# A graph pass's destination scores in fp32 with eight columns per step, instead of three bf16 parts

## The reference, cut to what matters

```
hh = (x @ W).reshape(n, H, D)
s_src = jnp.einsum('nhd,hd->nh', hh, a_src)
s_dst = jnp.einsum('nhd,hd->nh', hh, a_dst)
scores = jax.nn.leaky_relu(s_src[src] + s_dst[dst], negative_slope=0.2)
m = jax.ops.segment_max(scores, dst, num_segments=n)
e = jnp.exp(scores - m[dst])
denom = jax.ops.segment_sum(e, dst, num_segments=n)
out = jax.ops.segment_sum(hh[src] * (e / denom[dst])[:, :, None], dst, num_segments=n)
```

## Time and profile before

| | |
|---|---|
| runs | 5453.67, 5473.58, 5479.73 us |
| span of the profiled execution | 5404.7 us; the profile gives no other time for this execution, so what lies around the span is taken as the difference to the median, 68.9 us |
| the second graph's pass | about 2795 to 4190 us |
| busy over the span | PE 3933.5 us (73%), its weight loads 2847.1, DVE 3064.0 (57%), ACT 1859.8 (34%), POOL 2464.9 (46%) |
| L931, the gathers of this pass | 878.7 us, 880 of 999 ns |
| L967, the sums | 676.3 us busy, 1760 of 520 ns |

### The profile page before, as it was taken

One profiled execution on the slowest core, in us unless ns is written; L12 is line 12 of the kernel. 1 busy time (PEld: TensorE's weight loads), 2 busy tenths in 40 slices (PEclk: granted clock), 3 DMA queues, 4 the chain that ended last, 5 costly groups with the idle time before them and its releaser, 6 DMA issues. The chain is left out here.

```text
span 5404.7 us, 69347 instructions
## 1 busy us (share of the span) xinstructions
PE 3933.5 (73%) x16281; PEld 2847.1 (53%) x16282; DVE 3064.0 (57%) x7623; ACT 1859.8 (34%) x5073; POOL 2464.9 (46%) x2442
## 2 busy tenths in 40 slices
PE   6867777777777659967853666666666338999999
PEld 4545555555555448856732444444444226777776
DVE  3278887878888766662154666666667773111111
ACT  1333333333333312311222444444444322333332
POOL 2256665656666450001166666666663422333332
PEclk8988988888888879977986788777887559999999
DMA  2555555555555232211173333333331451111111
GB/s 80 186 146 149 154 151 148 151 140 153 147 148 151 83 118 84 91 55 40 52 252 89 95 96 96 94 95 94 93 96 47 127 194 20 32 32 31 31 31 27
DMA packets 316127, 553.64 MB, mean 102 GB/s; under 512 B 63431, under 2 KB 213783, under 8 KB 315857
## 3 DMA queue, kind: packets, MB, share of 16 engines
q0 software_dynamic: 137120, 388.63, 27.4%
q1 hardware_dynamic: 178736, 161.98, 9.8%
HBM read 459.75 MB, written 90.62 MB: 102 GB/s over the span
## 5 line engine op out<-in xcount | busy, mean ns | idle before, releaser
L427 POOL DMA_INDIRECT attend_ring<-kv_rows,all_step_src x880 | 860.1, 977 | 624.5 <-PE attend_ps_agg L468 371.3
L931 POOL DMA_INDIRECT edge_ring<-head_rows,all_step_src x880 | 878.7, 999 | 457.1 <-issue 204.2
L967 PE MATMUL edge_ps_agg<-edge_msg,edge_sel 128*128 128x264 f32 x1760 | 676.3, 520 | 188.9 <-issue 57.3
L468 PE MATMUL attend_ps_agg<-attend_msg,attend_sel 128*128 128x264 f32 x1760 | 605.1, 445 | 179.7 <-DVE graph_qa L785 122.9
L967 PEld LDWEIGHTS edge_ps_agg<-edge_msg,edge_sel 128*128 128x128 f32 x1760 | 414.5, 257 | 328.2 <-issue 198.7
L1266 DVE TENSOR_TENSOR graph_acc<-graph_acc,edge_ps_agg 128x264 f32 x880 | 369.9, 420 | 367.2 <-PE edge_ps_agg L967 169.0
L2821 DVE TENSOR_TENSOR moe_gl<-moe_ps_h,moe_act 128x341 f32<-128x341 f32 x210 | 107.8, 514 | 776.8 <-PE moe_ps_h L2739 776.8
L452 PE MATMUL attend_ps_q<-graph_qa,attend_sel_t 128*128 x1760 | 527.7, 429 | 27.4 <-ACT attend_sel_t L581 17.8
L785 DVE SCALAR_TENSOR_TENSOR graph_qa<-graph_qa,all_step_same,attend_ps_agg 128x264 f32 x880 | 421.1, 479 | 170.1 <-remote 121.0
L468 PEld LDWEIGHTS attend_ps_agg<-attend_msg,attend_sel 128*128 128x128 f32 x1760 | 329.3, 208 | 347.2 <-issue 148.6
L2739 PE MATMUL moe_ps_h<-experts_w,moe_xt 128*128 x1680 | 501.7, 451 | 0.6 <-ACT moe_xt L2770 0.6
(11 more groups left out here) (424 smaller groups left out, 6587.9 us busy)
## 6 DMA issues: line engine op xcount, KB each, us to landing
attend_ring<-kv_rows,all_step_src POOLq DMA_INDIRECT x880
edge_ring<-head_rows,all_step_src POOLq DMA_INDIRECT x880
kv_rows<-qkv_kv SPq DMA_DIRECT2D x25, 512.0 KB, 2.9
experts_w<-in_w_t SPq DMA_DIRECT2D x16, 682.0 KB
attend_mask<-run_starts SPq DMA_DIRECT2D x440, 8.1 KB
edge_mask<-run_starts SPq DMA_DIRECT2D x440, 8.1 KB
head_rows<-hds_hh SPq DMA_DIRECT2D x25, 264.0 KB
qkv_x<-in_x SPq DMA_DIRECT2D x25, 256.0 KB, 3.3
```

Of the source, the lines that this page charges most:

```text
L427: nc.gpsimd.indirect_dma_start(ring[:, step % RING1, :], None, g.kv_rows, bass.IndirectOffsetOnAxis(g.step_src[:, step:step + 1], 0)).then ...
L468: nc.tensor.matmul(ps_agg[i % SUM_BANKS][:, 0:AGG], sel[:, q % 2, u % QU, :], msg[:, q % 2, u % QU, :], start=True, stop=True).then_inc(s_ ...
L931: nc.gpsimd.indirect_dma_start(ring[:, n % slots, u, :], None, g.head_rows, bass.IndirectOffsetOnAxis(g.step_src[:, step:step + 1], 0)).th ...
L967: nc.tensor.matmul(ps_agg[i % BANKS][:, 0:AGG], sel[:, q % 2, u % QU, :], msg[:, q % 2, u % QU, :], start=True, stop=True).then_inc(s_agg, 1)
```

## The change

The three bf16 parts go. The one-hot matrices `sel_t` and the table are fp32, a step gives eight columns, and the 128 columns of a chunk go into one of two PSUM banks in turn. VectorE's reduction goes, and `both_parts` reads the bank itself. With seven banks used before, all eight are used now.

```
-        dst_parts = m.sb("dst_parts", [P, BLOCKS, H, PARTS], BF16)
-        rest = m.sb("rest", [P, BLOCKS, H])
-        sel_t = m.sb("sel_t", [P, 2, QU, P], BF16)
+        sel_t = m.sb("sel_t", [P, 2, QU, P])
-        dst_sum = m.sb("dst_sum", [P, CH, H])
-        ps_sd = m.ps("ps_sd", [P, CH, H, PARTS])
+        ps_sd = [m.ps(f"ps_sd{i}", [P, CH, H]) for i in range(2)]
...
-                if q == 0 and c >= 1:
-                    pe.wait_ge(s_sum, c)
+                if q == 0 and c >= 2:
+                    pe.wait_ge(s_v, (c - 2) * V_OPS + 1)
                 pe.wait_ge(s_rt, c * quarters + q + 1)
                 for u in range(QU):
-                    ins = nc.tensor.matmul(ps_sd[:, q * QU + u].rearrange("p h a -> p (h a)"), sel_t[:, q % 2, u, :],
-                                           dst_parts[:, bass.ds(blocks[(q * QU + u) % U], 1)].rearrange("p b h a -> p (b h a)"),
+                    ins = nc.tensor.matmul(ps_sd[c % 2][:, q * QU + u], sel_t[:, q % 2, u, :],
+                                           dst_vals[:, bass.ds(blocks[(q * QU + u) % U], 1), :].rearrange("p b h -> p (b h)"),
                                            start=True, stop=True)
...
-            ch.after(nc.vector.tensor_copy(rest[:], dst_vals[:]))
-            for p in range(PARTS):
-                ch.after(nc.vector.tensor_copy(dst_parts[:, :, :, p], rest[:]))
-                if p < PARTS - 1:
-                    ch.after(nc.vector.tensor_tensor(rest[:], rest[:], dst_parts[:, :, :, p], ALU.subtract))
...
-            def dst_part(a):
-                v.wait_ge(s_sd, (a + 1) * quarters)
-                nc.vector.tensor_reduce(dst_sum[:].rearrange("p u h -> p (u h)"), ps_sd[:].rearrange("p u h a -> p (u h) a"), AX.X, ALU.add).then_inc(s_sum, 1)
-
             def both_parts(a):
                 v.wait_ge(landed[a % slots], (a // slots + 1) * (16 * CH))
-                v.wait_ge(s_sum, a + 1)
+                v.wait_ge(s_sd, (a + 1) * quarters)
                 if a >= 1:
                     v.wait_ge(s_turned, a)
-                nc.vector.tensor_tensor(score[:].rearrange("p h u -> p u h"), dst_sum[:], ring[:, a % slots, :, D:AGG], ALU.add).then_inc(s_v, 1)
+                nc.vector.tensor_tensor(score[:].rearrange("p h u -> p u h"), ps_sd[a % 2][:], ring[:, a % slots, :, D:AGG], ALU.add).then_inc(s_v, 1)
...
             def turn(a, b):
                 at = rows_of(b, 0)
                 message(b, 0, 1, 2, 3)
-                dst_part(a)
                 message(b, 4, 5)
```

More of the change, by code:

```diff
@@ L52 @@
 QBANKS, SUM_BANKS = 3, 2
-PARTS = 3
 CHUNKS_OF = HALVES * U // CH
@@ L890, in edges @@
         s_set, s_made, s_gt, s_rt, s_sd, s_off, s_rs = (m.sem(k) for k in ("set", "made", "gt", "rt", "sd", "off", "rs"))
-        s_sum, s_score, s_turned, s_runs, s_row, s_v, s_carry, s_less = (
-            m.sem(k) for k in ("sum", "score", "turned", "runs", "row", "v", "carry", "less"))
+        s_score, s_turned, s_runs, s_row, s_v, s_carry, s_less = (
+            m.sem(k) for k in ("score", "turned", "runs", "row", "v", "carry", "less"))
         s_ends, s_drop, s_grown, s_small, s_shrink, s_prob_t, s_prob = (
@@ L899, in edges @@
         by_head = lambda t: t.rearrange("p (h u) -> p h u", h=H)
-        V_OPS, LOADS, SET_OPS = 8, 12, 10
+        V_OPS, LOADS, SET_OPS = 8, 12, 4
         @block.sync
```

## The result

The changed kernel took 5515.2 us (median of six, 5509.2 to 5521.2) against 5473.9 for the kernel before, timed beside it: 1.0085 of it, 95% interval 1.0064 to 1.0105. That is 41 to 46 us slower, depending on whether one takes the medians or the ratio, where I had forecast +12. A second comparison gave 1.0089 (1.0063 to 1.0116).

What follows compares the result with a forecast made beforehand. It took a turn to be two holds and the gathers between them, with neither PE nor DVE pacing. Set-up -3.4 and +1.2, steady turns +13, drain +1.5 sum to +12.3 us: about 5486 us, range 5425 to 5575.

Steps and rivals of the forecast that it cites:

- the likeliest case: Whole kernel: the turn's rhythm is kept, +12.3 us, time about 5486, chance 0.47.
- rival 1: Steady turns: delayed matmul results miss a hold, more turns run long; one in four gives about 5539; chance 0.33.
- What bounds the kernel: Steady turn: two holds and the gathers between them; neither PE nor DVE paces it; turns 23.9 us.
- TensorE's price: at_node in fp32: +1.13 us a quarter, 4.5 us a turn, 249 us in all if nothing hid it.
- What of it reaches the end: Added TensorE work per turn: bounds 0 and 1.5 us, taken 0.25, from two equal 23.90 us turns; +13 us.
- Quarter by quarter: at_node's four quarters: 0 to 0.7 us stick out, then 0.5, none, and a gain in length of only 0.34.
- My answer for the third: Third quarter of at_node: lies wholly in PE's 4.01 us stand before L953, so hidden.
- VectorE's reduction at 0: dst_part on VectorE: 30.2 us of busy time go, but become idle time, 0 in the steady turns.
- L1156 from PSUM at 0: VectorE's both_parts, L1169 before, reads PSUM instead of SBUF: between -4.6 and +10.2 us in all, taken 0.
- Set-up and drain: Second pass's ends: set-up -3.4 us for six DVE operations, +1.2 for the first at_node; last two turns +1.5.
- The second (VectorE counts in full): VectorE: 30.2 + 3.4 us saved in full, PE stays hidden, time 5440; chance 0.15.
- the third by the stops: Steady turns: fewer holds as POOL is stopped sooner, a turn could approach 21 us; chance 0.05 with unknown gains.

Runs made afterwards that it cites:

- set 2: Four kernels, each the kernel before with one quarter's at_node in fp32: 1.0003, 0.9997, 0.9963, 1.0007; the kernel before took 5035.6 us there.
- fp32 with the reduction kept: Kernel before with one-hots and table in fp32, still 24 columns a step, one bank, VectorE's reduction kept: 1.0090, +49 us.
- three bf16 matmuls: Changed kernel, but three bf16 parts of the scores added up in PSUM by three 8-column matmuls a step: 1.0144, +78 us over the kernel before.
- The moved second quarter: Changed kernel with the second quarter's at_node and its place_t moved behind the row transposes on TensorE: 1.0089 of the kernel before.
- the four kernels made for it: Kernel before with only the first, second, third or fourth quarter's at_node in fp32: 1.0003, 0.9997, 0.9963, 1.0007.
- the single bf16 part: Changed kernel with a bf16 table copy and one bf16 matmul a step, two lower parts left out, no reduction: 1.0013, +7 us.

## Why the prediction was off

The sign of the likeliest case held and the size did not: +12.3 forecast, +41 to 49 measured. That is above the 0.5% within which I put the most chance, and inside the range. It lies there partly by luck: I had stretched the range upwards for rival 1, whose mechanism isn't the one that was measured.

- *What bounds the kernel.* Right in kind: a turn is GpSimd's gathers and its stops. With gathers taken out the turn drops from 24.0 to 17.5 us, and PE's added work then counts almost in full. I had only the last two turns for this, and they spoke true. In the regime of set 2 the turn is the gathers alone, 20.7 us, near the 21 that I had worked out for them. That nothing of TensorE's length reaches the stops was wrong.
- *TensorE's price.* 4.5 us a turn estimated, 3.8 measured as busy time (3.6 without gathers). Right to a fifth.
- *What of it reaches the end.* **The step that failed**: "I take 0.25, near the lower end, because that row is the very thing measured." It came to 46 / 53 = 0.9 us in the timed runs, and 1.2, 0.5 and 0.7 in the profiles of the changed kernel, of the same kernel again and of fp32 with the reduction kept: inside my bounds of 0 to 1.5, and well above 0.25. The two turns of 23.90 us in the earlier trace rows, on which I built it, were two picked out of 51. Take all 51 turns of that trace, from one L974 to the next: the half with less PE time has 14.9 us of it and takes 23.6 us, the half with more has 16.2 and takes 24.4. So 1.3 us more of PE went along with 0.8 us more of turn, where my pair said 2 us for nothing. This doesn't prove that the one causes the other, but it takes away the ground for a value near 0. The stand before L953 was 143.3 us over 52 turns, 2.8 us each, and it is gone in the changed kernel. Without gathers there is none, and 3.0 of 3.6 us show. I read it as what hid part of the work, but that is argued and doesn't hold as a sum: three bf16 matmuls added 1.5 us a turn, less than the stand, and cost 1.4; and in set 2, with hardly such a stand, one quarter in fp32 cost nothing. How much of added work is hidden, and where, stays open.
- *Quarter by quarter.* My answer for the third ("lies wholly in the 4.01 us stand") took a stand of one turn for a fixed thing. With the other quarters longer it comes in another place and is shorter. The moved second quarter cost the same. Which quarter is exposed was not settled, because the four kernels made for it ran where completions are in time.
- *VectorE's reduction at 0, L1156 from PSUM at 0.* Both right: fp32 costs 1.0090 with the reduction and 1.0085 and 1.0089 without; the removal alone gave 1.0013. L1156 takes 362 ns against 364. By the Trainium skill, Perfetto Trace Analysis, section Identifying the Most-Contended Engine, the engine with the highest occupancy is to be optimised first. POOL is the highest with 16.0 of 24 us, and taking its gathers away did save 6%. VectorE had 15.6, close to it, and relieving that one gained nothing.
- *Set-up and drain.* The set-up is as forecast: the six operations are gone, and the last small memsets follow each other at once.

```profile
2835.02 0.07 DVE L1141 MEMSET edge_so_far<- 1x8 f32 x1
2835.35 0.91 DVE L1143 MEMSET edge_keep<- 1x1024 f32 x1 [0.27 <-DVE edge_so_far L1141]
```

  The first quarter took 2860.16 - 2858.44 = 1.72 us for my 1.64. The drain is mis-sized: 20.4 and 18.3 us against 17.9 and 17.1, so +3.7 for my +1.5. Without gathers nearly all of the added work shows there too.

```profile
2858.44 1.87 PE L949 MATMUL edge_ps_sd<-graph_s_dst,edge_sel_t 128*128 x8 [28.12 <-ACT edge_sel_t L1065]
2860.16 0.59 PE L940 MATMUL edge_ps_gt<-edge_feat,all_lane_feat 128*128 128x512 bf16 x1
```

- *The rivals.* The first had the right side and nearly the right time (5539), but not its mechanism: it wanted turns of 28 us among unchanged ones of 23.9. Turns of 27 us or more did rise in the profiled execution, from 2 to 6 of 51, but the second profile of the same kernel has none, and its median turn is 24.7 against 23.9 before. It is the usual turn that grew. The second (VectorE counts in full) is refuted by the single bf16 part, the third by the stops, which became more.

## What to carry to other kernels

Don't take two turns for a rule. When two of them say that extra work on an engine is swallowed, set busy time against length over all turns of the trace; here that would have warned me. Then find the stand that could swallow the work, add it up over the loop and divide by the turns. It is a first guess and not a budget: 2.8 us a turn of stand hid about three quarters of 3.8 us, and almost nothing of the 1.5 us that three bf16 matmuls added. To price a change to one engine of a pipeline, do its part alone and the other engine's part alone: two runs gave +0.90% and +0.13% here, and settled who paid. Before subtracting two profiles, compare a stretch that the change doesn't touch: here the first graph's pass differed by 42 us. Check as well whether the pipeline's pace is the same from one set of runs to the next, before turning a wait of one trace into a rule.

## What the runs showed of the hardware

- While GpSimd issued gathers back to back, VectorE stood long for transposes that TensorE had, as I read it, already done, in the runs where the kernel before took 5415 to 5474 us: 21.97 us before one copy, 28.7 in the changed kernel, and between 4.4 (three bf16 matmuls) and 36.4 us (fp32 with the reduction) in the others. Where it took 5036 us the same copy stood 1.7 to 3.0 us in the four kernels, with the same gathers 1.26 us apart. The pass has turns of 24.0 us in the one and 20.7 in the other, and the DMAs moved 92 and 109 GB/s. What makes the difference I don't know; both regimes were seen under the same chip number. In the latter a turn is GpSimd's time alone, 16 x (0.99 + 0.30) us. The chain without gathers is 20.5 us in the changed kernel, so it should just fit under it; that was not run.
- An fp32 matmul of 8 columns with its own 128x128 weights, as here with an address from a register, costs 0.39 us a step at half clock (1.57 / 4). Three bf16 ones with the same weights cost 0.17 (0.68 / 4) there and 0.08 at full clock (0.31 / 4) against fp32's 0.22, and the kernel still lost by it.
